# Mix layer: the second residual from the centred rows, by Pool and DVE, in place of identity products on PE

## What is computed

```python
x1 = layer_norm(t + x, ln1_g, ln1_b)          # t: linear attention, x: the normalised rows
h = gelu(x1 @ W1.T + b1)
y = h @ W2.T + b2
return layer_norm(y + x1, ln2_g, ln2_b)       # y + x1 is the second residual
```

## Time and profile before

| what | value |
|---|---|
| median of 3 runs (lowest, highest) | 1179.63 us (1175.21, 1183.61) |
| the profiled execution: its own time, its span | 1178.52 us, 1176.8 us |
| busy share of the span: PE, DVE, ACT, POOL | 80%, 67%, 49%, 56% |
| mean granted TensorE clock (1 is 2.4 GHz) | 0.887 |
| stretch of the loop in which all its calls run, s = 4 to 24 | 141 to 310.7 us |

### The profile page before, as it was taken

One profiled execution on the slowest core, in us unless ns is written; L12 is line 12 of the kernel. 1 busy time (PEld: TensorE's weight loads), 2 busy tenths in 40 slices (PEclk: granted clock), 3 DMA queues, 4 the chain that ended last, 5 costly groups with the idle time before them and its releaser, 6 DMA issues. The chain is left out here.

```text
span 1176.8 us, 18595 instructions
## 1 busy us (share of the span) xinstructions
PE 943.8 (80%) x5483; PEld 677.4 (58%) x5483; DVE 788.3 (67%) x1644; ACT 582.4 (49%) x1539; POOL 661.5 (56%) x804
## 2 busy tenths in 40 slices
PE   2987799999984778787878777878757646999996
PEld 2876577777752444444444444444437645888885
DVE  7443356565634888888888887888839848665244
ACT  0442587878633666666666666666621112222220
POOL 4702455556556777777777777777706448552000
PEclk9999899999995888878888888888858877999998
DMA  8992232322337777777777777777617332110003
GB/s 217 160 214 105 80 115 105 113 108 108 113 130 227 236 237 236 238 228 236 234 235 239 235 238 229 233 238 234 212 48 242 114 120 75 55 32 1 1 1 109
DMA packets 99042, 186.21 MB, mean 158 GB/s; under 512 B 16867, under 2 KB 66406, under 8 KB 98942
## 3 DMA queue, kind: packets, MB, share of 16 engines
q0 software_dynamic: 39696, 129.88, 35.4%
q1 hardware_dynamic: 59246, 55.13, 16.8%
HBM read 147.59 MB, written 37.37 MB: 157 GB/s over the span
## 5 line engine op out<-in xcount | busy, mean ns | idle before, releaser
L1245 POOL DMA_INDIRECT big<-kv_scratch,src_i x392 | 371.6, 948 | 125.1 <-issue 116.6
L1486 DVE TENSOR_TENSOR big<-big,ps 128x1024 f32<-128x1024 f32 x98 | 119.2, 1216 | 62.2 <-DMA big<-kv_scratch,src_i 62.2
L1402 PE MATMUL ps<-big,edge 128*64 128x256 f32 x784 | 135.3, 475 | 31.4 <-DVE big L1545 17.6
L1388 PE MATMUL ps<-edge 64*128 64x256 f32 x784 | 147.9, 509 | 5.2 <-DMA edge<-q_scratch 3.6
L1493 DVE TENSOR_REDUCE ps<-big 128x32 f32<-128x1024 f32 x98 | 119.4, 1218 | 0.1
L1388 PEld LDWEIGHTS ps<-edge 64*128 64x128 f32 x784 | 87.9, 242 | 48.9 <-issue 35.2
L1545 DVE TENSOR_TENSOR big<-big,ps 128x1024 f32<-128x1024 f32 x98 | 114.7, 1211 | 0.0
L1402 PEld LDWEIGHTS ps<-big,edge 128*64 128x64 f32 x784 | 61.6, 164 | 83.6 <-issue 39.7
L1309 ACT ACTIVATE edge<-edge 128x64 f32<-128x64 f32 x392 | 102.9, 334 | 0.0
L1932 PE MATMUL ps<-big 128*128 128x256 f32 (+1 forms) x416 | 93.3, 380 | 2.2 <-ACT big L1850 2.2
L1941 PE MATMUL ps<-big 128*128 128x256 f32 x400 | 89.1, 380 | 0.0
(11 more groups left out here) (324 smaller groups left out, 1927.9 us busy)
## 6 DMA issues: line engine op xcount, KB each, us to landing
edge<-q_scratch SPq DMA_DIRECT2D x196, 64.0 KB
big<-kv_scratch,src_i POOLq DMA_INDIRECT x392
big<-in_x SPq DMA_DIRECT2D x8, 640.0 KB, 5.7
agg_scratch<-big SPq DMA_DIRECT2D x16, 252.0 KB
xn_scratch<-big SPq DMA_DIRECT2D x5, 640.0 KB
cols_scratch<-big SPq DMA_DIRECT2D x5, 640.0 KB
mix_scratch<-big SPq DMA_DIRECT2D x25, 128.0 KB, 1.7
edge<-mix_scratch SPq DMA_DIRECT2D x1, 3200.0 KB, 11.5
```

Of the source, the lines that this page charges most:

```text
L1245: pool.indirect_dma_start(kv[:, s, k, :], None, kv_d[0:N, :], bass.IndirectOffsetOnAxis(ap=src_i[:, e:e + 1], axis=0)).then_inc(got[s], 16)
L1388: ins = pe.matmul(qr_ps[g % 2][:, (2 * hg + k) * D:(2 * hg + k + 1) * D], ohT[64 * hg:64 * hg + 64, g % 2, k * P:(k + 1) * P], qwin[64 * h ...
L1402: ins = pe.matmul(sum_ps[64 * hg:64 * hg + 64, :], oneh[:, s, k, hg * 64:hg * 64 + 64], kv[:, s, 2 * hg + k, D:2 * D], start=(k == 0), sto ...
L1486: dve.tensor_tensor(k_rows, k_rows, qr_ps[g % 2].rearrange("p (k d) -> p k d", d=D), ALU.mult).then_inc(pr, 1)
```

## The change

`mix_y` keeps its two W2 products and loses the two identity products. POOL gets a call `gained(s-2)` at the end of each step that multiplies `xh` by `ln1_g`, spread over the partitions, into a new buffer `x1g` of three tiles; it waits for `m_xh` of its tile and for `m_c` of the tile three before, and raises `m_xg`. ACT's `centre` waits for `m_xg` before it writes an `xh` buffer again. DVE's `residual` waits for `m_xg` too, adds `x1g` to the W2 product in PSUM, and then adds the shift, for which `ln1_b` is added once to `b2` in the first stage. Two more vectors are spread by SP, ahead of `wr`. `x1T` is still made, since W1 needs it.

```diff
--- before.py
+++ after.py
@@ -104,7 +104,8 @@
         wqT = sb("wqT", [P, C, D])
         w1T = sb("w1T", [P, C, D])
         w2T = sb("w2T", [P, C, D])
-        vec_names = ["L0_gnn_ln_g", "L0_gnn_ln_b", "L0_mix_ln2_g", "L0_mix_ln2_b", "L0_mix_b2", "L0_ffn_b2"]
+        vec_names = ["L0_gnn_ln_g", "L0_gnn_ln_b", "L0_mix_ln2_g", "L0_mix_ln2_b", "L0_mix_b2", "L0_ffn_b2",
+                     "L0_mix_ln1_g", "L0_mix_ln1_b"]
         vecs = {n: sb("v_" + n, [P, D]) for n in vec_names}
         wr = sb("wr", [P, D])
         br = sb("br", [P, 1])
@@ -209,6 +210,7 @@
         den = big.take(2, H)
         sts, mvs, rss = big.take(4, 6), big.take(4, 2), big.take(4, 2)
         nmr = big.take(2)
+        x1g = big.take(3, D)
         assert big.at <= mix_end
         tab_kv = edge.take(2, 2 * D)
         tab_q = edge.take(2, ETY * D)
@@ -422,7 +424,7 @@
         m_q, m_min, m_exp, m_kf, m_t, m_tx, m_r1, m_rs, m_xh, m_T, m_x1, m_h, m_g, m_y, m_c, m_r2, m_out = (
             sem(n) for n in ("mix_q", "mix_min", "mix_exp", "mix_kf", "mix_t", "mix_tx", "mix_rstd_1", "mix_shift", "mix_xh",
                              "mix_turned", "mix_x1", "mix_h", "mix_gelu", "mix_y", "mix_stats_2", "mix_rstd_2", "mix_out"))
-        vmx, pmx = sem("mix_step"), sem("mix_pool_step")
+        vmx, pmx, m_xg = sem("mix_step"), sem("mix_pool_step"), sem("mix_x1_gained")
         N_VEC = 1 + 1 + len(vec_names) + 8
 
         with nc.Block() as block:
@@ -605,6 +607,15 @@
                     cm(pool.tensor_scalar(rss[:, j, 1:2], mvs[:, j, 1:2], EPS_LN, None, ALU.add))
                     pool.tensor_tensor(rss[:, j, 0:1], rss[:, j, 1:2], nhalf[:, 0:1], ALU.pow).then_inc(done, 1)
 
+                def gained(t):
+                    if t is None:
+                        return
+                    if t.t == 0:
+                        pool.wait_ge(s_pri, 1)
+                    seen(pool, m_xh, t)
+                    seen(pool, m_c, t.at(-3))
+                    pool.tensor_tensor(x1g[:, t.t % 3, :], xh[:, t.k, :], vecs["L0_mix_ln1_g"][:, :], ALU.mult).then_inc(m_xg, 1)
+
                 load(Tile(0, 0, NS))
                 load(Tile(0, 1, NS))
                 pool.wait_ge(s_bad, 1)
@@ -616,6 +627,7 @@
                     roots(m.at(-1), m_tx, m_r1, 0)
                     roots(m.at(-4), m_c, m_r2, 1)
                     store_q(t.at(-1))
+                    gained(m.at(-2))
                 seen_all(pool, g_kvout, NS, 16)
                 seen_all(pool, g_qout, NS, 16)
                 pool.sem_inc(s_end, 1)
@@ -677,6 +689,7 @@
                         return
                     seen(act, m_rs, t)
                     seen(act, m_T, t.at(-2))
+                    seen(act, m_xg, t.at(-2))
                     act.activation(xh[:, t.k, :], tx[:, t.k, :], ACT.Identity, bias=nmr[:, t.k:t.k + 1],
                                    scale=rss[:, t.k, 0:1]).then_inc(m_xh, 1)
 
@@ -892,9 +905,6 @@
                     seen(pe, m_c, t.at(-1))
                     y_ps = ps[6][:, 0:D]
                     pe.matmul(y_ps, hT[:, t.k, 0:P], w2T[:, 0, :], start=True, stop=False)
-                    for ch in range(C):
-                        pe.matmul(y_ps[:, ch * P:(ch + 1) * P], x1T[:, t.t % 3, ch * P:(ch + 1) * P], ident[:, :],
-                                  start=False, stop=False, skip_group_check=True)
                     ins = pe.matmul(y_ps, hT[:, t.k, P:2 * P], w2T[:, 1, :], start=False, stop=True)
                     ins.then_inc(m_y, 1)
 
@@ -1019,6 +1029,7 @@
                     dve.wait_ge(s_bd, 16 * (P // DK) * (C + 1))
                     c(dve.tensor_tensor(vecs["L0_mix_ln2_b"][:, :], vecs["L0_mix_ln2_b"][:, :], vecs["L0_gnn_ln_b"][:, :],
                                         ALU.add))
+                    c(dve.tensor_tensor(vecs["L0_mix_b2"][:, :], vecs["L0_mix_b2"][:, :], vecs["L0_mix_ln1_b"][:, :], ALU.add))
                     c(dve.tensor_scalar(pri[:, :], pri[:, :], float(1.0 / np.sqrt(DK).astype(np.float32)), None, ALU.mult))
                     for ch in range(C):
                         m = bd_a[:, ch, :, :].rearrange("p t (h d) -> p t h d", d=DK)
@@ -1145,7 +1156,9 @@
                         return
                     seen(dve, m_y, t)
                     seen(dve, m_out, t.at(-2))
-                    cm(dve.tensor_tensor(x2m[:, t.k, :], ps[6][:, 0:D], vecs["L0_mix_b2"][:, :], ALU.add))
+                    seen(dve, m_xg, t)
+                    cm(dve.tensor_tensor(x2m[:, t.k, :], ps[6][:, 0:D], x1g[:, t.t % 3, :], ALU.add))
+                    cm(dve.tensor_tensor(x2m[:, t.k, :], x2m[:, t.k, :], vecs["L0_mix_b2"][:, :], ALU.add))
                     cm(dve.bn_stats(sts[:, 2 + t.k, :], x2m[:, t.k, :]))
                     dve.bn_aggr(mvs[:, 2 + t.k, :], sts[:, 2 + t.k, :]).then_inc(m_c, 1)
 
@@ -2198,7 +2211,7 @@
 
 _INS = ["x", "src", "dst", "edge_type_3", "node_type_6", "L0_gnn_Wk", "L0_gnn_Wq", "L0_gnn_bk",
         "L0_gnn_bv", "L0_gnn_Wv", "L0_gnn_relation_pri", "L0_gnn_Wm", "L0_gnn_ln_g", "L0_gnn_ln_b",
-        "L0_mix_b2", "L0_mix_ln2_g", "L0_mix_ln2_b", "L0_ffn_wr", "L0_ffn_br",
+        "L0_mix_b2", "L0_mix_ln1_g", "L0_mix_ln1_b", "L0_mix_ln2_g", "L0_mix_ln2_b", "L0_ffn_wr", "L0_ffn_br",
         "L0_ffn_w1", "L0_ffn_w2", "L0_ffn_b2"]
```

## The result

The changed kernel takes **1188.67 us** (median of 8 runs, 1186.61 to 1191.29) where the kernel before, beside it, takes 1180.89. The ratio is 1.0076, with the interval 1.0056 to 1.0095: 9.0 us slower (6.6 to 11.2), against a forecast of +11.6 and a time of 1190. The two medians themselves lie 7.8 us apart: a recorded ratio isn't the plain quotient of the two medians, and differs from it by up to 0.0023 in what follows. Differences are given by the recorded ratio, and by the medians too where the two tell different things. The profiled execution of after took 1190.58 us with a span of 1188.8. The two profiled executions lie 12.0 us of span apart, 4.3 more than the medians, because the one of before lies 2.4 us under its median here and the one of after 1.9 over its own. So a row tells what one part costs, and the runs tell the sum.

What follows compares the result with a forecast made beforehand. The prediction took the ring of waits over DVE and ACT as the bound, PE's ring 0.15 us behind. Terms 9.7 + 0.2 - 0.9 + 2.6 = +11.6 us on 1178.52 gave 1190.1 us, range 1184 to 1198.

Steps and rivals of the forecast that it cites:

- The ring and its price: Loop of waits per step, DVE's L1123 to L1115, ACT's chain, L1123 again; second DVE add costs 21 x 0.46 = +9.7 us.
- PE's products in the full steps: Removing the identity products, 0.44 us of PE a step, only lengthens PE's pause in the 21 full steps: nothing gained.
- a pause before `turn_in`: PE's idle time at L807 in a full step, forecast at about 0.8 us instead of 0.34.
- The last steps: From s = 25: +0.2 us for the add at s = 25, -0.9 us for the removed products at s = 27 and 28.
- POOL: `gained` behind L596 in each step, at most 1.21 us; POOL still back in time, so nothing in the sum.
- My rival of the lock: POOL's product locks out DVE's adds on the ring, about 0.4 us a step, 8.4 in all, so 1198.5; chance 0.1.
- The first stage: Two more spreads in SP's queue delay the load DVE waits for at L1072: +2.6 us, ends 0.9 and 4.0.
- My price of 1.32 us: Cost of one spread in SP's queue, from six equal spreads in 7.90 us; taken twice for +2.6 us.
- My rival of the free first stage: SP's queue may have room at 60 us, so the spreads cost at most 0.9 us; about 1188; chance 0.1.
- The median: Whole kernel: forecast 1190.1 us, +11.6 on the profiled execution of before at 1178.52.
- the likelier side at 0.56 to 0.41: Chance 0.56 that the whole kernel stays within 1% (up to 1191.4 us), against 0.41 for slower.

## Why the prediction was right

**The ring and its price: right.** The sum had 21 x 0.46 = 9.7 us; from s = 4 to 25, after takes 9.5 more and the add alone 9.2. The reading that carried it was the distance between two instructions and not a share: PE was busy 96% of the stretch and could still lose 9 us of work for nothing. DVE's part of the ring is shown by adding to it (+9.2) and taking off again (-9.5 with the shift on POOL). ACT's part rests on its rows, the 0.42 us that `elu` waits for it and 4.30 us of work in 4.39; no run took work off ACT.

**PE's products in the full steps: right at nothing**, -0.07 us when taken away alone. One detail was off. I forecast a pause before `turn_in` of about 0.8 us, 0.34 + 0.44; it is 1.14. I had left out that the longer step adds to it as well.

**The last steps: the sum right by luck, its parts too small.** I had +0.2 for the add and -0.9 for the products, -0.7 together. The whole change gives -0.74 behind s = 25. But the products alone are worth -1.7 there and the add alone +0.8: PE's relief counts in four steps, not in two, and the two errors cancel.

**POOL: right that it costs nothing**, and 0.75 us in place of the bound of 1.21, which was an upper end and no more. The Trainium skill, "SBUF — State Buffer", section "Who interferes with whom", has the lock between POOL and a DVE instruction with two SBUF inputs. The traces agree for 128x256, and show where no hold is seen: L1173 is held by 0.39 us beside a 128x256 product, while L1103 (L1104 where POOL has the shift), with one input from PSUM, keeps its 0.69 beside the same product, and the new add at 212.01 keeps 0.42 though a `roots` of 128x1 runs until 212.13. My rival of the lock had the right mechanism and the right price; it failed on place, since `gained` stands beside L1103 in the full steps, and no DVE instruction of the ring is longer there than before.

**The first stage: the least certain term, and still so.** I took +2.6 us with ends 0.9 and 4.0. In after the first eviction is 3.8 us later; SP's stretch between first spread and first store is 2.6 us longer, but that match is chance, as the table of SP shows. Timed alone, the two spreads cost 5.0 (3.1 to 7.0), centred above my upper end. My price of 1.32 us came from six equal spreads in 7.90 us, one execution's row: the same six take 9.45 us in after and 10.68 to 11.62 in the other four traces of the faster chips, so 1.6 to 1.9 each. And that doesn't add up with the whole: 9.5 and -0.7 from the table and 5.0 make 13.8, while the change costs 9.0 (6.6 to 11.2). Nothing that I ran explains the difference. What the rows of SP show is that I had taken one execution's queue for the kernel's: SP's first spread alone moves by 7 us from trace to trace. The stages behind the loop took 820.5 to 824.2 us in the six traces of the faster chips, so they may take up a part; that is a guess. On a chip where the first stage stands still for another cause no wait for the permutation is left in the trace and the time doesn't move clear of noise (-1.8 to +3.1). My rival of the free first stage forecast such a result, but for another reason, room in the queue, and no run shows that.

**The median.** 1188.7 against 1190.1 forecast. That it is so close is in part luck: I added 11.6 us to an execution that lies 2.4 under the later median of the kernel before, and the change is 3.8 less than 11.6 by the medians, 2.6 by the ratio. The two errors cancel to 1.4. The forecast difference of 11.6 lies just above the measured interval (6.6 to 11.2). The result lies just inside 1%, the likelier side at 0.56 to 0.41.

## What to carry to other kernels

In a loop of fixed orders, find the ring: follow one step from engine to engine until it comes back to its start, and compare the last wait with the distance that the same two instructions have where that wait is absent. Work taken off the busiest engine is worth nothing while that engine has a pause in the step, and work put on a ring is paid in every step, so a sum that is to be split over engines goes to the one that is on neither ring (here POOL: the same arithmetic, and 9.5 us less in the loop), as long as that engine has time left, which here it nearly had not. Of a load that something waits for, ask what stands behind it on its queue too: moved ahead, it only uncovered the stores.

## What the runs showed of the hardware

Chips differ. Three took 10% longer than the others for the kernel before; every trace taken on them shows 190 or 191 GB/s from 400 to 800 us, in the edge stage, where the others show 233 to 235. Each was met in one session, so whether it stays so isn't shown. The two-spread kernel on one chip of each kind, busy times from 400 to 800 us, the slower one first:

```profile
400.00:800.00 400.00, 296.42 (x1673) 169.63 (x1673) 283.77 (x366) 213.29 (x625) 242.62 (x256) 0.73 0.66 190
```

```profile
400.00:800.00 400.00, 316.99 (x2024) 183.31 (x2020) 334.85 (x435) 256.11 (x754) 299.23 (x317) 0.83 0.78 235
```

From s = 4 to 25 this kernel takes 177.75 us on one and 177.72 on the other, so a change in the loop can be judged on either. One in SP's queue in the first stage can't. What the first stage waits for between 41 and 61 us on the slower ones isn't shown ("remote" is all that the trace names). And the step from s = 2 to 3 takes 9.9 us instead of 8.28 in some executions of any kernel; its cause stayed open.
